# Double-buffered token tile, earlier layernorm and a later log/exp stage in an RWKV + FFN layer kernel

## The chip, the cores and the metric

One Trainium2 chip, 8 cores, one launch. Every core runs the same program on one sequence of the batch; the cores exchange nothing. The metric is the device time in microseconds of the slowest core, from the first to the last instruction with what little lies around them.

## The reference

Per sequence (4096 tokens of 1024 channels; the batch is 8), cut to what matters:

```python
xn = layernorm(x)                                  # over the 1024 channels, no scale or shift
k = xn @ Wk.T ; r = xn @ Wr.T ; v = r              # 1024 x 1024 each
y = wkv_scan(-exp(time_decay), time_first, k, v)   # recurrence over the tokens, per channel
attn = (sigmoid(r) * y) @ Wo.T
gate = xn @ (w_gate/127).T ; up = xn @ (w_up/127).T   # 3072 hidden, int32 weights
ffn = (silu(gate) * up) @ (w_down/127).T
out = x + attn + ffn
```

## The kernel before, in words

The program has two phases with a full barrier between them (`bd.fence()`). Phase 1 makes, for all tokens, the normalized input and the gated WKV output, and stores both to DRAM (`xn_s`, `outp_s`); it also transposes all weights and stores those of the FFN (`wgu_s`, `wdT_s`). Phase 2 (line 670 on, to L767) reads them back and does the FFN, the output projection and the sum. The change touches phase 1 alone.

There is no scheduler. `Build.op` appends each operation to the queue of its engine in the order in which the Python code calls it, and works out from the `Res` objects which semaphores it has to wait for. Each engine takes its own queue strictly in order, so a waiting instruction holds up all that stands behind it on that engine. The DMAs issued from SP stand in SP's queue in the same way, and those of GpSimd in POOL's; a DMA issue also waits for the last DMA on the same semaphore.

Phase 1 handles 16 chunks (`NC1`) of 256 tokens (`TT1`) in stages. For a chunk c:

- `stage_a_dma(c)`, L425: SP loads 1 MB of x into `x_tok`.
- `stage_a_stats(c)`: DVE takes BN_STATS and BN_AGGR (L433, L438) for two groups of 128 tokens, and ACT makes 1/sqrt(var+eps) as Ln and Exp of 128x1 (L443, L448). The second L438 writes the tile that the first L443 reads, so it waits for it.
- `stage_a_apply(c)`, L457: two DVE operations write the normalized bf16 tile `xn_tok` (a single buffer).
- `stage_a_post(c)`: TensorE transposes it into `psT` (L471, 16 transposes), ACT copies it to `xn_fm` (L478), SP stores it (L482). The text calls the 16 transposes T(c).
- `stage_b(c)`: TensorE makes k and r in four pairs of output blocks (L496). A pair is four groups of 8 matmuls, in the order psK, psR, psK, psR. `psK` and `psR` have two buffers each. Per pair ACT takes exp(k) (L506) and exp(-r) (L511), and DVE the product `S4` (L516), which sets `psR` free. At the end two small ACT copies (L526, L530).
- `stage_c_scans(c)`: 16 DVE scans (L540, L548). `stage_c_stt(c)`: 16 DVE operations (L561, L567) that make the denominator in `S6`.
- `stage_d(c)`: 16 ACT operations, Ln and Exp in turn (L576, L580), for the reciprocal of the denominator.
- `stage_e(c)`: 8 DVE operations (L590), one multiply on POOL into `outb` (L597), and the store of `outb` from SP (L603).

Beside the chunks, 64 units of weight preparation are dealt out, four per iteration, by `pp_drip`. A unit is a cast DMA from GpSimd into `pp_in` (two buffers), 8 transposes on TensorE (`psP`, L293, L321, L354), an ACT copy (L299 for Wo, L326 for gate and up, L360 for down) and, but for Wo, a store from `pp_stage` (two buffers) by SP (L331, L365). The load of a unit can be issued only when the transposes of the unit two before it are done, and an ACT copy into `pp_stage` waits for the store of the unit two before it. Units 0 to 7 are Wo (iterations 0 and 1), 8 to 55 gate and up (iterations 2 to 13), 56 to 63 down, with three groups of transposes and three copies each (iterations 14 and 15).

Iteration ch of the loop issues, in this order: the load for chunk ch+2, scans and stt of ch, stage e of ch-1, stage b of ch+1, stage d of ch, stats, apply and post of ch+2, and four units. T(2) is thus in iteration 0, T(15) in iteration 13, and from one T to the next are 13 intervals. Ahead of the loop stand stages a and b of chunk 0 and stage a of chunk 1.

Of the kernel before, what the change touches and what calls it, by code (L numbers as in the profile page):

```python
# [7 lines left out]
F32 = mybir.dt.float32  # L8
# [5 lines left out]
P = 128  # L14
C = 1024
# [108 lines left out]
def build_program(T=4096):  # L124
    TT1 = 256
    NC1 = T // TT1
    TS1 = TT1 // P
# [4 lines left out]
    nc = bass.Bass("TRN2", target_bir_lowering=False)  # L132
# [18 lines left out]
    bd = Build(nc)  # L151

    with contextlib.ExitStack() as top:
# [44 lines left out]
        with contextlib.ExitStack() as ph1:  # L198
            E1 = ph1.enter_context
            wkT = E1(nc.sbuf_tensor("wkT", [P, CC * C], BF16))  # L200
            wrT = E1(nc.sbuf_tensor("wrT", [P, CC * C], BF16))
            x_tok = [E1(nc.sbuf_tensor("x_tok0", [P, TS1 * C], F32))]
            xn_tok = [E1(nc.sbuf_tensor("xn_tok0", [P, TS1 * C], BF16))]
# [21 lines left out]
            r_wkT, r_wrT = Res("wkT"), Res("wrT")  # L225
            r_x_tok = [Res("x_tok0")]
            r_xn_tok = [Res("xn_tok0")]
# [11 lines left out]
            r_mv = [Res(f"mv{i}") for i in range(2)]  # L239
            r_stt = [Res(f"stt{i}") for i in range(2)]  # L240
# [15 lines left out]
            for i, v in [(0, EPS), (1, -0.5), (2, -1.0), (5, 127.0)]:  # L256
                bd.op("gpsimd", lambda e, i=i, v=v: e.memset(cst[:, i:i + 1], v),
                      writes=[r_cst])
# [162 lines left out]
            def stage_a_dma(ch):  # L421
                t0 = ch * TT1
                sl = ch % 2
                src = dram_ap(x_d, t0 * C, [[C, P], [P * C, TS1], [1, C]])
                bd.op("sync", lambda e, src=src: e.dma_start(out=x_tok[0][:], in_=src),  # L425
                      writes=[r_x_tok[0]], dma_sem="d_x0")

            def stage_a_stats(ch):
                sl = ch % 2
                for ts in range(TS1):  # L430
                    for hh in range(2):
                        bd.op("vector",
                              lambda e, sl=sl, ts=ts, hh=hh: e.bn_stats(  # L433
                                  stt_b[sl][:, (ts * 2 + hh) * 6:(ts * 2 + hh + 1) * 6],
                                  x_tok[0][:, ts * C + hh * 512: ts * C + (hh + 1) * 512]),
                              reads=[r_x_tok[0]], writes=[r_stt[sl]])
                    bd.op("vector",
# [15 lines left out]
            def stage_a_apply(ch):  # L453
                sl = ch % 2
                for ts in range(TS1):
                    bd.op("vector",
                          lambda e, sl=sl, ts=ts: e.tensor_scalar(  # L457
                              out=xn_tok[0][:, ts * C:(ts + 1) * C],
                              in0=x_tok[0][:, ts * C:(ts + 1) * C],
                              scalar1=mvb[sl][:, ts * 2:ts * 2 + 1], op0=ALU.subtract,  # L460
                              scalar2=rstd[sl][:, ts:ts + 1], op1=ALU.mult),
                          reads=[r_x_tok[0], r_mv[sl], r_rstd[sl]], writes=[r_xn_tok[0]])

# [141 lines left out]

            stage_a_dma(0)
            stage_a_stats(0)
            stage_a_apply(0)
            stage_a_post(0)
            stage_b(0)  # L610
            stage_a_dma(1)
            stage_a_stats(1)
            stage_a_apply(1)
            stage_a_post(1)
            while (pp_dma_idx < min(2, len(pp_units))
                   and pp_can_dma(pp_dma_idx, pp_idx)):
                pp_get(pp_dma_idx)[0]()
                pp_dma_idx += 1
            for ch in range(NC1):
                if ch + 2 < NC1:  # L620
                    stage_a_dma(ch + 2)
                stage_c_scans(ch, 0, CC)
                stage_c_stt(ch)
                if ch > 0:
                    stage_e(ch - 1)
                if ch + 1 < NC1:
                    stage_b(ch + 1)
                stage_d(ch)
                if ch + 2 < NC1:
                    stage_a_stats(ch + 2)  # L630
                    stage_a_apply(ch + 2)
                    stage_a_post(ch + 2)
                pp_drip((len(pp_units) * (ch + 1)) // NC1)
            stage_e(NC1 - 1)

# [171 lines left out]
```

How the kernel before makes its waits and increments, by code:

```python
        def emit(e, wl=wl, fn=fn, sem=sem, inc=inc):  # L77
            for s, v in wl:
                e.wait_ge(self.sems[s], v)
            inst = fn(e)
            inst.then_inc(self.sems[sem], inc)
# [10 lines left out]
        def emit(e, sem=sem, val=val):  # L92
            e.wait_ge(self.sems[sem], val)
```

## Time and profile before

| what | us |
|---|---|
| median of 3 runs | 2081.68 |
| lowest and highest | 2078.19, 2343.77 |
| the profiled execution, its own time | 2082.22 |
| its span on the slowest core (core 6) | 2080.7 |
| spans of the other seven cores | 2057.8 to 2078.0 |
| busy over the span: PE | 1537.6 (74%) |
| busy over the span: DVE | 629.4 (30%) |
| busy over the span: ACT | 465.4 (22%) |
| busy over the span: POOL | 122.3 (6%) |

The 1.5 us between the span and the execution's own time is what lies around the instructions. Busy shares are averages over two phases that have little in common: phase 1 takes the first 798 us or so, phase 2 the rest. The times of the rows below are microseconds from the start of the span. In a timeline a row is: start, duration, engine, line, operation, output and inputs, count, and in brackets the idle time of the engine before it with what ended it. PE is TensorE, DVE VectorE, ACT ScalarE, POOL GpSimd, SPq and POOLq the queues that issue DMAs.

### The profile page before, as it was taken

The page shows a single profiled execution, that of the slowest core. Times are in us where ns is not written, and L with a number is a line of the kernel's source. Part 1 is how long each engine was busy: PE and PEld are TensorE (multiplying, and loading weights), DVE is VectorE, ACT ScalarE, POOL GpSimd, SP SyncE. Part 2 cuts the span into 40 slices and gives each one's busy share as a digit, 9 for nine tenths or more (in the row PEclk, how much of TensorE's full clock was granted, in tenths as well). Part 3 has the DMA queues.
Part 4 walks back from the last instruction along what each step waited for, and adds up shares of the span by engine and source line. Part 5 has one row for each costly group of instructions (what it writes and reads, how often), then busy time and mean ns, then how long its engine had stood idle before and what let it go on. Part 6 is the DMA issues. An engine that isn't in the chain of part 4 may idle for free.

```text
span 2080.7 us, 24779 instructions; the slowest of 8 cores (2057.8 to 2080.7 us)
## 1 busy us (share of the span) xinstructions
PE 1537.6 (74%) x8192; PEld 801.9 (39%) x8192; DVE 629.4 (30%) x1094; ACT 465.4 (22%) x803; POOL 122.3 (6%) x112
## 2 busy tenths in 40 slices
PE   2554455446544423998998998998998998998995
PEld 2443444335444311433433433433433433433432
DVE  0455776676667510201201201201201201201201
ACT  3334444544443331100100100100100100100100
POOL 1011112112111110000000000000000000000000
PEclk9867678767777655999999999999999999999998
DMA  6323455355445477647647747647647648648641
GB/s 100 73 61 61 91 118 117 81 107 110 109 86 105 100 141 187 152 122 207 156 122 206 159 122 208 157 122 210 158 122 211 154 121 212 157 120 214 153 121 62
DMA packets 573611, 280.59 MB, mean 135 GB/s; under 512 B 477232, under 2 KB 526384, under 8 KB 573488
## 3 DMA queue, kind: packets, MB, share of 16 engines
q1 hardware_dynamic: 557744, 237.05, 45.1%
q0 software_dynamic: 15744, 41.95, 10.9%
q8 instruction: 71, 1.16, 0.2%
q14 instruction: 52, 0.43, 0.1%
HBM read 251.70 MB, written 52.43 MB: 146 GB/s over the span
## 4 chain that ended last, share of the span: by engine, by line
PE 71%; DMA 11%; ACT 7%; issue 6%; DVE 4%; SPq 0%; POOL 0%; ACTq 0%; DVEq 0%; POOLq 0%
PE psA L699 17%; PE psB L710 16%; PE psRb L740 9%; PE psR L496 6%; PE psK L496 6%; DMA pp_in<-wu 4%; PE psB L740 4%; PE psA L740 4%; PE psRb L752 3%; DMA pp_in<-wd 3%; ACT S L580 3%; ACT S L576 2%; DVE res L761 1%; PE psB L752 1%; PE psA L752 1%
## 5 line engine op out<-in xcount | busy, mean ns | idle before, releaser
L699 PE MATMUL psA<-xnc,wgu 128*128 128x512 bf16 x1536 | 375.6, 389 | 58.3 <-DVE res L761 29.6
L710 PE MATMUL psB<-xnc,wgu 128*128 128x512 bf16 x1536 | 367.4, 382 | 0.0
L718 ACT ACTIVATE sil<-psA,cst 128x512 f32<-128x512 f32 x192 | 131.9, 687 | 1036.2 <-PE psA L699 1036.2
L723 DVE SCALAR_TENSOR_TENSOR h_sb<-sil,cst,psB 128x512 bf16<-128x512 f32 x192 | 143.6, 748 | 597.8 <-PE psB L710 597.8
L699 PEld LDWEIGHTS psA<-xnc,wgu 128*128 128x128 bf16 x1536 | 152.3, 100 | 248.8 <-issue 75.1
L710 PEld LDWEIGHTS psB<-xnc,wgu 128*128 128x128 bf16 x1536 | 151.7, 99 | 186.7 <-issue 9.7
L740 PE MATMUL psRb<-wdt,h_sb 128*128 128x512 bf16 x768 | 196.4, 377 | 36.5 <-DVE h_sb L723 8.9
L761 DVE TENSOR_TENSOR res<-psRb,x 128x512 f32<-128x512 f32 x32 | 22.1, 692 | 525.6 <-PE psB L752 523.1
L471 PE MATMUL psT<-identsb,xn_tok 128*128 128x128 bf16 x256 | 29.8, 308 | 177.5 <-DVE xn_tok L457 177.5
L496 PE MATMUL psK<-xn_fm,wkT 128*128 128x256 bf16 x1024 | 150.2, 295 | 4.8 <-ACT xn_fm L478 3.1
L496 PE MATMUL psR<-xn_fm,wrT 128*128 128x256 bf16 x1024 | 145.9, 290 | 6.9 <-DVE S L516 6.9
L740 PEld LDWEIGHTS psRb<-wdt,h_sb 128*128 128x128 bf16 x768 | 61.4, 96 | 171.6 <-issue 125.7
L496 PEld LDWEIGHTS psK<-xn_fm,wkT 128*128 128x128 bf16 x1024 | 108.0, 106 | 24.8 <-issue 5.5
L496 PEld LDWEIGHTS psR<-xn_fm,wrT 128*128 128x128 bf16 x1024 | 106.4, 104 | 26.6 <-issue 8.0
L321 PE MATMUL psP<-identsb,pp_in 128*128 128x128 bf16 x384 | 46.8, 307 | 91.3 <-DMA pp_in<-wg 76.6
L740 PE MATMUL psB<-wdt,h_sb 128*128 128x512 bf16 x384 | 114.2, 379 | 0.0
L740 PE MATMUL psA<-wdt,h_sb 128*128 128x512 bf16 x384 | 114.2, 379 | 0.0
L471 PEld LDWEIGHTS psT<-identsb,xn_tok 128*128 128x128 bf16 x256 | 26.0, 142 | 181.5 <-issue 181.5
L540 DVE TENSOR_TENSOR_SCAN zDb<-dv,zDb,S 128x256 f32<-128x256 f32 x128 | 93.1, 728 | 0.0
L548 DVE TENSOR_TENSOR_SCAN zNb<-dv,zNb,S 128x256 f32<-128x256 f32 x128 | 92.8, 725 | 0.0
L516 DVE TENSOR_TENSOR S<-S,psR 128x512 f32<-128x512 f32 x64 | 43.8, 686 | 135.2 <-PE psK L496 81.3
L767 POOL DMA_DIRECT2D out<-res x8 | 6.0, 755 | 1277.3 <-DVE res L761 1277.3
(58 smaller groups left out, 1125.1 us busy)
## 6 DMA issues: line engine op xcount, KB each, us to landing
wgu<-wgu_s SPq DMA_DIRECT2D x192, 512.0 KB, 5.0
wdt<-wdT_s SPq DMA_DIRECT2D x192, 256.0 KB, 2.6
x_tok<-x SPq DMA_DIRECT2D x16, 1024.0 KB, 7.2
x<-x SPq DMA_DIRECT2D x8, 2048.0 KB, 15.5
out<-res POOLq DMA_DIRECT2D x8, 2048.0 KB, 8.6
wgu_s<-pp_stage SPq DMA_DIRECT2D x48, 256.0 KB, 6.0
xn_s<-xn_fm SPq DMA_DIRECT2D x16, 512.0 KB, 6.5
outp_s<-outb SPq DMA_DIRECT2D x16, 512.0 KB, 3.6
```

The costliest lines, as they stand in the source:

```text
L321: last = e.transpose(psP[sl][:, cc * P:(cc + 1) * P], pp_in[sl][:, cc * P:(cc + 1) * P], ident[:])
L471: last = e.transpose(psT[ts][:, cc * P:(cc + 1) * P], xn_tok[0][:, ts * C + cc * P: ts * C + (cc + 1) * P], ident[:])
L496: last = e.matmul(psx[pk][:, half * TT1:(half + 1) * TT1], wT[:, cc_i * C + cc_o * P: cc_i * C + (cc_o + 1) * P], xn_fm[sl][:, cc_i * TT1: ...
L540: lambda e, sl=sl, ol=ol, cc=cc, b0=b0: e.tensor_tensor_scan(out=zDb[sl][:, b0 + 1: b0 + 1 + TT1], data0=bass.AP(dv, cc, [[CC, P], [0, TT1]]),
L548: lambda e, sl=sl, ol=ol, cc=cc, b0=b0: e.tensor_tensor_scan(out=zNb[sl][:, b0 + 1: b0 + 1 + TT1], data0=bass.AP(dv, cc, [[CC, P], [0, TT1]]),
L580: lambda e, sl=sl, sli=sli: e.activation(out=S6[sl][:, sli], in_=S5[sl][:, sli], func=AF.Exp, scale=cst[:, 2:3]),
L699: last = e.matmul(psA[pab][:], wgu_t[wsl][:, (iu * CC + cc) * P:(iu * CC + cc + 1) * P], xnc[sl][:, cc * TT2:(cc + 1) * TT2], start=(cc == ...
L710: last = e.matmul(psB[pab][:], wgu_t[wsl][:, (iu * CC + cc) * P:(iu * CC + cc + 1) * P], xnc[sl][:, cc * TT2:(cc + 1) * TT2], start=(cc == ...
L718: lambda e, pab=pab: e.activation(out=sil_b[pab][:], in_=psA[pab][:], func=AF.Silu, scale=cst[:, 3:4]),
L723: lambda e, hc=hc, pab=pab: e.scalar_tensor_tensor(out=h_sb[:, hc * TT2:(hc + 1) * TT2], in0=sil_b[pab][:], scalar=cst[:, 4:5], in1=psB[pa ...
L740: last = e.matmul(bank_t[ts * 2 + dh][:], h_sb[:, hc * TT2 + ts * P: hc * TT2 + (ts + 1) * P], wd_t[wsl][:, dh * 512:(dh + 1) * 512], star ...
L752: last = e.matmul(bank_t[ts * 2 + dh][:], otc[sl][:, hc2 * TT2 + ts * P: hc2 * TT2 + (ts + 1) * P], woT[:, hc2 * C + dh * 512: hc2 * C + ( ...
```

## The change

`x_tok` gets a second buffer, with its own semaphore, and the load of x runs one chunk further ahead (ch+3 in iteration ch). In the loop, stats and apply of chunk ch+2 move from behind stage d to the head of the iteration, ahead of the scans; `stage_a_post(ch+2)` stays behind stage b; and stage d of ch moves from before them to the very end of the iteration, behind the four weight units.

```diff
-            x_tok = [E1(nc.sbuf_tensor("x_tok0", [P, TS1 * C], F32))]
+            x_tok = [E1(nc.sbuf_tensor(f"x_tok{i}", [P, TS1 * C], F32)) for i in range(2)]
...
-                bd.op("sync", lambda e, src=src: e.dma_start(out=x_tok[0][:], in_=src),
-                      writes=[r_x_tok[0]], dma_sem="d_x0")
+                bd.op("sync",
+                      lambda e, sl=sl, src=src: e.dma_start(out=x_tok[sl][:], in_=src),
+                      writes=[r_x_tok[sl]], dma_sem=f"d_x{sl}")
...
             stage_a_dma(0)
+            stage_a_dma(1)
             stage_a_stats(0)
             stage_a_apply(0)
             stage_a_post(0)
             stage_b(0)
-            stage_a_dma(1)
+            stage_a_dma(2)
             stage_a_stats(1)
             stage_a_apply(1)
             stage_a_post(1)
...
             for ch in range(NC1):
+                if ch + 3 < NC1:
+                    stage_a_dma(ch + 3)
                 if ch + 2 < NC1:
-                    stage_a_dma(ch + 2)
+                    stage_a_stats(ch + 2)
+                    stage_a_apply(ch + 2)
                 stage_c_scans(ch, 0, CC)
                 stage_c_stt(ch)
                 if ch > 0:
                     stage_e(ch - 1)
                 if ch + 1 < NC1:
                     stage_b(ch + 1)
-                stage_d(ch)
                 if ch + 2 < NC1:
-                    stage_a_stats(ch + 2)
-                    stage_a_apply(ch + 2)
                     stage_a_post(ch + 2)
                 pp_drip((len(pp_units) * (ch + 1)) // NC1)
+                stage_d(ch)
             stage_e(NC1 - 1)
```

The reads of `x_tok[0]` in stats and apply become reads of `x_tok[sl]` with sl the parity of the chunk. In the changed kernel lines behind L427 are numbered one higher, and those behind the loop three higher.

ScalarE's queue in the kernel before, around the end of iteration 1 and the start of iteration 2 (stage d is eight such pairs and four unit copies stand in a row, of which one pair and two copies are shown; the digit behind a name is the buffer):

```order
L576 ACTIVATE S5_1<-S6_1 128x256
L580 ACTIVATE S6_1<-S5_1,cst 128x256
L443 ACTIVATE lnv1<-mvb1,cst 128x1
L448 ACTIVATE rstd1<-lnv1,cst 128x1
L478 COPY xn_fm1<-psT0 128x8x128
L478 COPY xn_fm1<-psT1 128x8x128
L299 COPY woT<-psP0 128x8x128
L299 COPY woT<-psP1 128x8x128
L506 ACTIVATE S1_1<-psK0 128x512
```

ScalarE's queue in the changed kernel at the turn from one iteration to the next (L326 are the unit copies, L577 and L581 are stage d, L444 and L449 the Ln and Exp of the statistics, L507 is the first evacuation of stage b):

```order
L326 COPY pp_stage1<-psP0 128x1024
L326 COPY pp_stage0<-psP1 128x1024
L577 ACTIVATE S5_0<-S6_0 128x256
L581 ACTIVATE S6_0<-S5_0,cst 128x256
L444 ACTIVATE lnv1<-mvb1,cst 128x1
L449 ACTIVATE rstd1<-lnv1,cst 128x1
L507 ACTIVATE S1_0<-psK0 128x512
```

Before, stage d stood ahead of the statistics, the `xn_fm` copies and the units of its iteration; now it stands behind its iteration's units, and the statistics of the next iteration stand behind it.

VectorE's queue in the kernel before, at the turn from iteration 1 to iteration 2 (L590 is stage e of chunk 0, L516 the `S4` product of chunk 2, L433 to L457 the layernorm of chunk 3, L540 the first scan of chunk 2):

```order
L590 SCALAR_TENSOR_TENSOR S5_0<-S4_0,euv,zNb0 128x256 x8
L516 TENSOR_TENSOR S4_0<-S1_0,psR0 128x512
L516 TENSOR_TENSOR S4_0<-S1_0,psR1 128x512
L433 BN_STATS sttb1<-x_tok0 128x6 x2
L438 BN_AGGR mvb1<-sttb1 128x2
L457 TENSOR_SCALAR xn_tok0<-x_tok0,mvb1,rstd1 128x1024 x2
L540 SCALAR_TENSOR_TENSOR zDb0<-dv,zDb1,S1_0 128x256
```

VectorE's queue in the changed kernel, at the turn from iteration 2 to iteration 3 (L591 is stage e of chunk 1, L517 `S4` of chunk 3, L434 to L458 the layernorm of chunk 5, L541 the first scan of chunk 3):

```order
L591 SCALAR_TENSOR_TENSOR S5_1<-S4_1,euv,zNb1 128x256 x8
L517 TENSOR_TENSOR S4_1<-S1_1,psR0 128x512
L517 TENSOR_TENSOR S4_1<-S1_1,psR1 128x512
L434 BN_STATS sttb1<-x_tok1 128x6 x2
L439 BN_AGGR mvb1<-sttb1 128x2
L458 TENSOR_SCALAR xn_tok0<-x_tok1,mvb1,rstd1 128x1024 x2
L541 SCALAR_TENSOR_TENSOR zDb1<-dv,zDb0,S1_1 128x256
```

On VectorE the kinds of work follow each other as before; what differs is the chunk: the layernorm that stands ahead of the scans of chunk c is that of chunk c+2 instead of c+1.

## Rows read from the trace of the kernel before

**Rows 1.** Waits between 60 and 860 us: waiting, released by, total us, times, longest.

```profile
PE psT L471 <- DVE xn_tok L457: 172.6, 15, 12.0
ACT pp_stage L326 <- DMA wgu_s<-pp_stage: 123.1, 21, 8.2
```

**Rows 2.** Timeline of one iteration, all engines, 411 to 455 us.

```profile
411.25 1.73 DVE L457 TENSOR_SCALAR xn_tok<-x_tok,mvb,rstd 128x1024 bf16<-128x1024 f32 x2 [0.95 <-ACT rstd L448]
...
413.13 1.86 PE L471 MATMUL psT<-identsb,xn_tok 128*128 128x128 bf16 x16 [11.99 <-DVE xn_tok L457]
...
414.23 2.17 ACT L478 COPY xn_fm<-psT 128x1024 bf16<-128x1024 bf16 x2 [3.16 <-PE psT L471]
...
430.89 1.01 ACT L326 COPY pp_stage<-psP 128x1024 bf16<-128x1024 bf16 x1 [4.97 <-DMA wgu_s<-pp_stage]
...
433.80 0.68 DVE L516 TENSOR_TENSOR S<-S,psR 128x512 f32<-128x512 f32 x1
...
443.77 0.41 ACT L576 ACTIVATE S<-S 128x256 f32<-128x256 f32 x1
...
451.04 0.28 ACT L443 ACTIVATE lnv<-mvb,cst 128x1 f32<-128x1 f32 x1
...
452.71 1.73 DVE L457 TENSOR_SCALAR xn_tok<-x_tok,mvb,rstd 128x1024 bf16<-128x1024 f32 x2 [1.01 <-ACT rstd L448]
```

**Rows 3.** Busy time of each engine in the stretch 413.1 to 454.6 us.

```profile
413.10:454.60 41.50, 21.88 (x177) 18.55 (x178) 27.44 (x53) 18.71 (x36) 6.69 (x5) 0.71 0.47 102
```

**Rows 4.** Instructions on the tile x_tok: who waited, us in total, times.

```profile
DMA x_tok<-x: 13.3, 1
```

**Rows 5.** Timelines of PE and ACT: transposes of some chunks, with the iteration's last unit copy.

```profile
125.74 1.87 PE L471 MATMUL psT<-identsb,xn_tok 128*128 128x128 bf16 x16 [11.70 <-DVE xn_tok L457]
...
141.90 1.01 ACT L299 COPY woT<-psP 128x1024 bf16<-128x1024 bf16 x1 [4.36 <-PE psP L293]
...
253.00 1.86 PE L471 MATMUL psT<-identsb,xn_tok 128*128 128x128 bf16 x16 [11.70 <-DVE xn_tok L457]
...
266.64 1.01 ACT L326 COPY pp_stage<-psP 128x1024 bf16<-128x1024 bf16 x1 [2.10 <-DMA wgu_s<-pp_stage]
...
332.56 1.86 PE L471 MATMUL psT<-identsb,xn_tok 128*128 128x128 bf16 x16 [11.69 <-DVE xn_tok L457]
...
352.08 1.01 ACT L326 COPY pp_stage<-psP 128x1024 bf16<-128x1024 bf16 x1 [5.33 <-PE psK L496]
...
659.92 1.86 PE L471 MATMUL psT<-identsb,xn_tok 128*128 128x128 bf16 x16 [11.70 <-DVE xn_tok L457]
...
682.29 1.01 ACT L326 COPY pp_stage<-psP 128x1024 bf16<-128x1024 bf16 x1 [8.06 <-PE psR L496]
```

**Rows 6.** Timeline of iteration 0, 85 to 106 us.

```profile
85.13 1.73 DVE L457 TENSOR_SCALAR xn_tok<-x_tok,mvb,rstd 128x1024 bf16<-128x1024 f32 x2 [1.37 <-ACT rstd L448]
...
88.11 2.17 ACT L478 COPY xn_fm<-psT 128x1024 bf16<-128x1024 bf16 x2 [3.58 <-PE psT L471]
...
104.52 1.28 DVE L516 TENSOR_TENSOR S<-S,psR 128x512 f32<-128x512 f32 x2
```

**Rows 7.** Timeline of the end of phase 1, 691 to 794 us.

```profile
691.56 1.06 PE L354 MATMUL psP<-identsb,pp_in 128*128 128x128 bf16 x16
...
702.96 0.59 POOL L343 DMA_DIRECT2D pp_in<-wd  x1 [17.20 <-PE psP L354]
...
741.66 4.53 POOL L597 TENSOR_TENSOR outb<-S 128x2048 bf16<-128x2048 f32 x1
...
750.59 0.48 DVE L590 SCALAR_TENSOR_TENSOR S<-S,euv,zNb 128x256 f32<-128x256 f32 x1 [0.42 <-ACT S L580]
...
753.35 0.59 POOL L343 DMA_DIRECT2D pp_in<-wd  x1 [7.17 <-PE psP L354]
...
792.08 1.01 ACT L360 COPY pp_stage<-psP 128x1024 bf16<-128x1024 bf16 x1 [2.01 <-DMA wdT_s<-pp_stage]
793.73 0.48 SPq L603 DMA_DIRECT2D outp_s<-outb  x1
```

More of the change, by code:

```diff
@@ L225, in build_program @@
             r_wkT, r_wrT = Res("wkT"), Res("wrT")
-            r_x_tok = [Res("x_tok0")]
+            r_x_tok = [Res(f"x_tok{i}") for i in range(2)]
             r_xn_tok = [Res("xn_tok0")]
@@ L434, in stage_a_stats @@
                                   stt_b[sl][:, (ts * 2 + hh) * 6:(ts * 2 + hh + 1) * 6],
-                                  x_tok[0][:, ts * C + hh * 512: ts * C + (hh + 1) * 512]),
-                              reads=[r_x_tok[0]], writes=[r_stt[sl]])
+                                  x_tok[sl][:, ts * C + hh * 512: ts * C + (hh + 1) * 512]),
+                              reads=[r_x_tok[sl]], writes=[r_stt[sl]])
                     bd.op("vector",
@@ L458, in stage_a_apply @@
                               out=xn_tok[0][:, ts * C:(ts + 1) * C],
-                              in0=x_tok[0][:, ts * C:(ts + 1) * C],
+                              in0=x_tok[sl][:, ts * C:(ts + 1) * C],
                               scalar1=mvb[sl][:, ts * 2:ts * 2 + 1], op0=ALU.subtract,
                               scalar2=rstd[sl][:, ts:ts + 1], op1=ALU.mult),
-                          reads=[r_x_tok[0], r_mv[sl], r_rstd[sl]], writes=[r_xn_tok[0]])
+                          reads=[r_x_tok[sl], r_mv[sl], r_rstd[sl]], writes=[r_xn_tok[0]])
             def stage_a_post(ch):
```

## The prediction

> **What bounds the kernel now.** I read the rows in the order of the questions. First, who waits for whom in phase 1: the transposes of a chunk wait for the normalized tile for 172.6 us in 15 waits, and the unit copies of ScalarE wait for their stores for 123.1 us [rows 1]. The first looks like what the change goes for. Then one iteration in order of time shows why the transposes wait [rows 2]. After its last evacuation of stage b ScalarE runs stage d (from 443.77), and only behind it the Ln and Exp of the statistics (451.04). Apply follows at 452.71, the transposes at 454.59, and TensorE had been idle for 11.7 us before each T that I looked at [rows 5]. On VectorE the same row, apply, stands ahead of the scans, stt and stage e, and behind those stands the `S4` product that frees `psR` for the later pairs of stage b (433.80).
>
> So the loop that sets the period of 41 us is: apply, scans, stt, stage e, first `S4`, rest of stage b, stage d, Ln and Exp, apply. No engine is full: in 41.5 us PE is busy 21.88, DVE 27.44, ACT 18.71 (the PE, DVE and ACT entries of the row) [rows 3]. From T(2) at 125.74 to T(15) at 659.92 are 13 intervals, 534.2 us, 41.1 each [rows 5].
>
> **The x tile.** On `x_tok` somebody waited once in the whole run, 13.3 us, for the first load [rows 4]. The second buffer and the earlier issue therefore remove nothing, and the load costs nothing on SP: it is issued at the same place as before, behind the last `wgu_s` store of an iteration, and its buffer has been free since the apply of an iteration earlier. I take 0. The first load would still have to land, so the 13.3 us stay. The Trainium skill, in Trainium Kernel Development and Optimization, section Best Practices, says to double-buffer so that DMA overlaps with compute. By that rule this edit would gain time; the trace has no such wait to remove after the first, so it changes nothing.
>
> **What the reordering removes.** T(ch+2) no longer waits for apply, which has run an iteration's length earlier. It starts when stage b ends. That takes 11.7 us of idle time from TensorE. But nothing downstream is bound by that alone.
>
> **What it adds.** The Ln and Exp of the next layernorm now stand behind stage d on ScalarE, and stage d stands behind the four unit copies. On VectorE the scans still stand behind apply. So scans(ch+1) wait for: T(ch+2), its copies, the four units with their DMAs, stage d(ch), Ln and Exp of ch+3, apply(ch+3). Before, the units ran beside the 22 us of scans, stt and stage e; that cover is gone, since VectorE stands idle until the units and stage d are done. And stage b of ch+2 can do two of its four pairs and then waits in `psR` for `S4`, which waits for all of it. Everything behind it waits too: the next T, and with it the next units. I add up the interval from T to T:
>
> - From T to the end of the last unit copy. In [rows 5]: 141.90+1.01-125.74 = 17.2 for the first iteration; 14.65 is the least of 13 (253.00 to 267.65), 20.5 the largest (332.56 to 353.09). The mean of iterations 0 to 12 is 18.4, and the iteration of [rows 2] has 18.8. The long part is DMA: the loads of the last two units can only be issued when the first two have been transposed, and the last copy waits for the store of the second unit [rows 2]. These transfers stand in the same order in both kernels. I take 18.4.
> - Stage d: 443.77 to 451.04, 7.3 [rows 2].
> - Ln, Exp and the ping-pong with BN_AGGR: 451.04 to 452.71, 1.7 [rows 2].
> - Apply, scans, stt and stage e, up to the first `S4`: 411.25 to 433.80, 22.5 [rows 2].
> - From the first `S4` to the end of stage b, where TensorE has stood at `psR`: iteration 0 of the kernel before has such a case. `S4` starts at 104.52 [rows 6], and stage b ends at 125.74-11.70 = 114.04 [rows 5]: 9.5.
>
> The sum is 59.4 us against 41.1, 18.3 us more in each of 13 intervals: +238.
>
> **Ahead of them.** In iteration 0 statistics and apply of chunk 2 come between apply(1) and the first scan. ScalarE is busy with the copies of T(1) until 88.11+2.17 = 90.3; then come 1.7 for Ln and Exp and 1.65 for apply, so the scans start at 93.6. Before, they started at 85.13+1.65 = 86.8 [rows 6]. Stage b(1) ends 6.8 later, at 120.8, and T(2) stands there instead of at 125.74: -4.9.
>
> **Behind them.** After T(15) there is no apply. In iteration 13 the last unit copy ended 23.4 after T [rows 5]. Stage d(13) then runs to 30.7; stage e(13) writes what it reads and so ends with it; exp(k) and exp(-r) of the first pair, half the width of a unit copy each and so some 0.65 us by estimate, take 1.3 more; 9.5 to the end of b(15): 41.5, where it was 691.56-659.92 = 31.6 [rows 5, 7]. In exchange stage d(14) no longer stands ahead of the first copies of unit 56, whose following load was issued 11.4 after stage b ended (702.96) [rows 7] and now some 4.1 after by estimate (three groups of transposes and a copy at 1.0 each [rows 7]): at 45.6 instead of 43.0 after T(15), +2.5. Stage d(14) falls into the wait for the load of unit 60, at the place where d(15) stood before (to 750.5), but the POOL multiply of chunk 14 now follows it: 751.1+0.2+4.53 = 755.8, and the load behind it on POOL's queue, issued at 753.35 before, goes out 2.6 later [rows 7]. Last, d(15) stands bare at the end: from 793.1 on 7.3 of stage d, 0.6 for the last L590, 4.7 for the multiply, 0.3 to the issue: the last `outp_s` store is issued at 806.0 instead of 793.73 [rows 7], +12.3, and the barrier to phase 2 waits for it. Together +17.4. Phase 2 is the same code and gets the same inputs: 0.
>
> **Sum.** -4.9 + 238 + 17.4 = +250.5 on the profiled execution's 2082.2, which lies 0.5 above the median of the runs shown: 2333.
>
> **Rivals.**
> - The transfers shrink. The 18.4 us are mostly waits for DMA, and with a longer interval the queues could be emptier, so that four copies of 1.0 follow the `xn_fm` copies (which end at 416.40, 3.3 after T [rows 2]) at once: 7.3 in place of 18.4. Then an interval is 48.3 and the kernel 2333-13x11.1 = 2189, still slower. Against it: these DMAs wait for each other within one iteration, which a longer interval does not change. 7 in 100.
> - The period stays at 41.1 and the idle time only moves from T to `psR`: 2082-4.9+17.4 = 2095, within 2%. It would need scans that don't wait for the late Ln and Exp. The queue of VectorE speaks against it: apply stands ahead of the first scan. 3 in 100.
> - Faster. If stage d ran inside the waits of ScalarE between the unit copies, the 11.7 us of TensorE would go and nothing take their place: 13x11.7 = 152 less, 2082-5-152+17 = 1942. For it speaks that no engine is over 27.44 busy in 41.5 [rows 3]; against it, ScalarE takes its queue in order and stage d is behind the copies. 2 in 100.
> - The forecast, in which ScalarE's queue ties units and scans into one loop, holds 88 in 100. It costs time from the point where T to last copy is longer than 41.1-41.0 = 0.1 us (41.0 is the sum of the other four terms), so no shortening of the transfers alone can turn it.
>
> **How the numbers follow.** The unknown is how long the units take in the new rhythm. With the least value (14.65) in each interval the sum falls by 13x3.7 = 49 to 2284; with the largest (20.5) it rises by 28 to 2361, and with the 23.4 of iteration 13 by 65 to 2398. The range is 2275 to 2385. A measurement of this kernel can tell about 2% from no change; by the cases faster is 0.02, the same 0.03, slower 0.95.
>
> **What would show it.** In the changed profile the wait of L472 for `xn_tok` should be gone; T to T should be 57 to 62 us; VectorE should stand some 20 us idle ahead of the second BN_AGGR (L439), released by ScalarE; ScalarE's first evacuation L507 should follow L449 directly; TensorE should have two idle stretches, for the unit loads and over 20 us at psR (L497) for `S4`. Phase 2 should keep its length. I am wrong if L439 waits only a few us, if intervals are under 50, or if the last unit copy comes under 10 us after T.

## The result, and the profile after

The changed kernel takes 2318.47 us in the median of 10 runs (lowest 2299.62), the kernel before 2081.65 us. The ratio is 1.1098 with a 95% interval from 1.1054 to 1.1143: 11% slower. The profiled execution has a span of 2298.1 us on its slowest core (core 4) against 2080.7. Most kernels here have some runs that are disturbed and far longer; the ratios leave them out, the medians do not.

The difference of 217.4 us between the two spans lies in phase 1. The starts of the transposes T and the first load of phase 2 cut both profiles into the same parts:

| part | before | after | difference | predicted |
|---|---|---|---|---|
| start to T(2) | 125.7 | 124.2 | -1.5 | -4.9 |
| T(2) to T(15), 13 intervals | 534.2 | 743.4 | +209.2 | +238 |
| T(15) to the first load of phase 2 | 138.4 | 148.5 | +10.2 | +17.4 |
| phase 2 | 1282.4 | 1282.0 | -0.4 | 0 |

Before, an interval was 41.1 us; now it is 57.2. First the waits of the changed kernel between 60 and 1030 us (waiting, released by, us in total, times, longest), which answer to [rows 1]:

```profile
PE psR L497 <- DVE S L517: 289.1, 14, 22.3
DVE mvb L439 <- ACT lnv L444: 247.3, 14, 20.4
...
ACT pp_stage L326 <- DMA wgu_s<-pp_stage: 108.0, 20, 6.1
PE psK L497 <- ACT S L507: 105.5, 14, 8.9
...
PE psT L472 <- DVE xn_tok L458: 13.4, 2, 8.5
```

The wait of the transposes for the normalized tile is gone, as intended: 13.4 us in two waits, both ahead of the loop, where there were 172.6 in 15. In its place TensorE waits 289 us for `S4` to free `psR`, in 14 waits of up to 22.3, and VectorE 247 us for the Ln of the statistics. The wait of the unit copies for their stores is about as long as before (108.0 against 123.1). It is the same wait, and yet it now costs what it did not cost then, since VectorE stands idle behind it.

The timeline of one interval of the changed kernel, which answers to [rows 2]:

```profile
577.68 1.06 PE L472 MATMUL psT<-identsb,xn_tok 128*128 128x128 bf16 x16
...
578.73 2.17 ACT L479 COPY xn_fm<-psT 128x1024 bf16<-128x1024 bf16 x2
...
593.64 1.01 ACT L326 COPY pp_stage<-psP 128x1024 bf16<-128x1024 bf16 x1 [3.96 <-PE psK L497]
...
594.54 0.42 ACT L577 ACTIVATE S<-S 128x256 f32<-128x256 f32 x1
...
601.82 0.28 ACT L444 ACTIVATE lnv<-mvb,cst 128x1 f32<-128x1 f32 x1
...
602.26 0.21 DVE L439 BATCH_NORM_AGGREGATE mvb<-sttb 128x2 f32<-128x12 f32 x1 [19.40 <-ACT lnv L444]
603.02 0.29 ACT L449 ACTIVATE rstd<-lnv,cst 128x1 f32<-128x1 f32 x1
603.22 0.58 ACT L507 ACTIVATE S<-psK 128x512 f32<-128x512 f32 x1
...
603.91 1.73 DVE L458 TENSOR_SCALAR xn_tok<-x_tok,mvb,rstd 128x1024 bf16<-128x1024 f32 x2 [1.43 <-ACT S L507]
...
626.46 1.28 DVE L517 TENSOR_TENSOR S<-S,psR 128x512 f32<-128x512 f32 x2
...
627.28 1.86 PE L497 MATMUL psR<-xn_fm,wrT 128*128 128x256 bf16 x8 [21.48 <-DVE S L517]
...
635.49 1.06 PE L472 MATMUL psT<-identsb,xn_tok 128*128 128x128 bf16 x16
```

Read from top to bottom it is the loop of the prediction. The transposes start without idle time ahead of them. The last unit copy ends 17.0 us later (594.65), stage d runs 7.2 us behind it, Ln, aggregate and Exp 2.1, and only then does apply run. VectorE has stood still for 19.4 us at the second BN_AGGR, and ScalarE's first evacuation (603.22) follows the last Exp of the statistics directly. The first `S4` comes 22.55 after apply begins, TensorE has been waiting 21.48 us in `psR`, and 9.0 us after `S4` starts the next transposes begin. 17.0 + 7.2 + 2.1 + 22.55 + 9.0 adds up to this interval, 57.8 with the second decimals.

The busy time of each engine over the 13 intervals (stretch, its length, then PE, PEld, DVE, ACT, POOL busy with their counts, the granted clock of TensorE as a share, DMA share, GB/s), first of the kernel before and then of the changed one:

```profile
125.70:659.90 534.20, 275.98 (x2288) 236.51 (x2289) 356.55 (x677) 242.63 (x468) 86.98 (x65) 0.74 0.47 99
```

```profile
124.20:867.60 743.40, 293.93 (x2290) 232.62 (x2289) 355.00 (x676) 237.65 (x469) 86.91 (x65) 0.68 0.32 70
```

VectorE's work is the same in both, 357 and 355 us. No engine is busy longer but PE, by 18 us for the same instructions: its granted clock fell from 0.74 to 0.68 in the mean. Behind the wait of 21.48 us in `psR` the clock is at the lower of its two levels (1.2 GHz) for most of the next 4.7 us and then at the upper one (2.4 GHz); the granted clock is the third entry from the end, 0.54 and 1.00:

```profile
627.30:632.00 4.70, 4.70 (x25) 3.33 (x25) 0.44 (x1) 0.60 (x1) 3.96 (x1) 0.54 0.00 0
632.00:635.50 3.50, 3.50 (x35) 3.14 (x33) 0.69 (x1) 1.28 (x2) 0.00 (x0) 1.00 0.51 154
```

TensorE's work behind the first `S4` is part of the loop, and the 9.0 us hold these slower rows, as the 9.5 of the forecast did. The rest of the loss is idle time.

### The profile page after: what moved, and what is told of

It reads as the page before. It is cut to its first block, busy times and chain, and to the rows that moved or that the text cites. A ratio compares the mean times of both kernels' runs of the same rounds, so it can differ in the third digit from the quotient of the medians.

```text
span 2298.1 us, 24717 instructions; the slowest of 8 cores (2287.1 to 2298.1 us)
## 1 busy us (share of the span) xinstructions
PE 1548.6 (67%) x8089; PEld 797.8 (35%) x8192; DVE 627.7 (27%) x1094; ACT 460.4 (20%) x803; POOL 122.2 (5%) x112
## 3 DMA queue, kind: packets, MB, share of 16 engines
q1 hardware_dynamic: 557744, 237.05, 40.4%
## 4 chain that ended last, share of the span: by engine, by line
PE 59%; DMA 12%; DVE 11%; issue 10%; ACT 7%; POOL 0%; DVEq 0%; ACTq 0%; SPq 0%; POOLq 0%
PE psA L702 15%; PE psB L713 15%; PE psRb L743 8%; DMA wgu_s<-pp_stage 5%; PE psR L497 4%; PE psB L743 4%; PE psA L743 3%; PE psK L497 3%; PE psRb L755 3%; ACT S L581 2%; DVE S L562 2%; DVE S L568 2%; ACT S L577 2%; DMA pp_in<-wd 2%; DVE S L591 2%
## 5 line engine op out<-in xcount | busy, mean ns | idle before, releaser
L497 PE MATMUL psR<-xn_fm,wrT 128*128 128x256 bf16 x1024 | 164.2, 314 | 289.1 <-DVE S L517 289.1
L497 PE MATMUL psK<-xn_fm,wkT 128*128 128x256 bf16 x1024 | 172.9, 325 | 108.6 <-ACT S L507 105.5
L497 PEld LDWEIGHTS psR<-xn_fm,wrT 128*128 128x128 bf16 x1024 | 113.8, 112 | 322.0 <-issue 294.8
L497 PEld LDWEIGHTS psK<-xn_fm,wkT 128*128 128x128 bf16 x1024 | 117.2, 116 | 142.2 <-issue 112.6
L743 PEld LDWEIGHTS psRb<-wdt,h_sb 128*128 128x128 bf16 x768 | 61.4, 96 | 171.6 <-issue 125.7
L507 ACT ACTIVATE S<-psK 128x512 f32<-128x512 f32 x64 | 37.9, 593 | 392.8 <-PE psK L497 392.8
L598 POOL TENSOR_TENSOR outb<-S 128x2048 bf16<-128x2048 f32 x16 | 72.0, 4502 | 539.6 <-DVE S L591 539.6
L541 DVE TENSOR_TENSOR_SCAN zDb<-dv,zDb,S 128x256 f32<-128x256 f32 x128 | 93.1, 727 | 0.0
L439 DVE BATCH_NORM_AGGREGATE mvb<-sttb 128x2 f32<-128x12 f32 x32 | 6.7, 209 | 289.8 <-ACT lnv L444 288.0
L321 PE MATMUL psP<-identsb,pp_in 128*128 128x128 bf16 x384 | 36.8, 262 | 67.3 <-DMA pp_in<-wg 56.2
L517 DVE TENSOR_TENSOR S<-S,psR 128x512 f32<-128x512 f32 x64 | 42.7, 684 | 142.4 <-PE psK L497 89.8
```

Source lines behind the costliest of these rows:

```text
L497: last = e.matmul(psx[pk][:, half * TT1:(half + 1) * TT1], wT[:, cc_i * C + cc_o * P: cc_i * C + (cc_o + 1) * P], xn_fm[sl][:, cc_i * TT1: ...
L541: lambda e, sl=sl, ol=ol, cc=cc, b0=b0: e.tensor_tensor_scan(out=zDb[sl][:, b0 + 1: b0 + 1 + TT1], data0=bass.AP(dv, cc, [[CC, P], [0, TT1]]),
L598: bd.op("gpsimd", lambda e, sl=sl: e.tensor_tensor(out=outb[0][:], in0=S5[sl][:], in1=S6[sl][:], op=ALU.mult), reads=[r_s5[sl][cc] for cc ...
L743: last = e.matmul(bank_t[ts * 2 + dh][:], h_sb[:, hc * TT2 + ts * P: hc * TT2 + (ts + 1) * P], wd_t[wsl][:, dh * 512:(dh + 1) * 512], star ...
```

## The experiments

All kernels were timed beside the kernel before on the same chip. T to T below is (T(15)-T(2))/13 in each profile.

**The buffer alone.** The kernel before with the second `x_tok` and the earlier load; the two lines ahead of the loop are as in the change.

```diff
 # the order of the kernel before, but:
-                if ch + 2 < NC1:
-                    stage_a_dma(ch + 2)
+                if ch + 3 < NC1:
+                    stage_a_dma(ch + 3)
                 stage_c_scans(ch, 0, CC)
```

> The kernel before with the second x_tok buffer and the load one chunk further ahead, nothing else moved. Loop theory (the loss comes from the order on ScalarE and VectorE, not from the buffer): period stays 41 us, the start is some 3 us longer because two loads of x now stand beside the first weight loads; 2082 to 2090 us. Rival (the extra early load contends with the unit transfers in each iteration): over 2110.

Measured: median 2084.15 us, ratio 1.0004 (0.9980 to 1.0029), T to T 41.1. The buffer and the load gain and cost nothing that can be measured; the transposes wait as before (the 16th wait is T(0), which lies ahead of the window in the kernel before):

```profile
PE psT L472 <- DVE xn_tok L458: 177.5, 16, 12.0
```

**Stage d put back.** The changed kernel, with stage d behind stage b again.

```diff
                 if ch + 1 < NC1:
                     stage_b(ch + 1)
+                stage_d(ch)
                 if ch + 2 < NC1:
                     stage_a_post(ch + 2)
                 pp_drip((len(pp_units) * (ch + 1)) // NC1)
-                stage_d(ch)
```

> The changed kernel with stage d put back where it stood before (behind stage b, ahead of post and the units); statistics and apply stay at the head of the iteration. Loop theory (it is the Ln and Exp behind the four unit copies that closes the loop, wherever stage d stands on ScalarE in between): from the end of stage b 1.2 + stage d 7.3 + xn_fm copies and units up to some 24.5, Ln and Exp 1.7, 22.5 to the first S4, 9.5 to the end of stage b: a period of 58, 2290 to 2330 us. Rival (the late stage d is the cause): back to 2085 or less.

Measured: 2252.99 us, ratio 1.0844 (1.0801 to 1.0886), T to T 54.7. The late stage d is not the main cause: without it most of the loss, 8.4 of 11.0%, is still there, and VectorE still waits for the Ln and TensorE for `S4` (between 60 and 1000 us):

```profile
PE psR L497 <- DVE S L517: 288.9, 15, 22.3
DVE mvb L439 <- ACT lnv L444: 212.8, 14, 19.1
```

My number missed: I had expected 58, not 54.7. The miss lies in one term: from the end of stage b to the last unit copy I took 24.5 us, with stage d and the units as a plain sum, and in the profile it is 21.2 in the mean of the 13 intervals. Part of stage d lies beside transfers: the loads of the last two units are issued at its start, while the first copies, and the stores behind them, still wait for its end. T is at 554.10, stage d runs from 555.14 to 562.52, and the last copy ends 23.2 after T:

```profile
555.14 0.42 ACT L577 ACTIVATE S<-S 128x256 f32<-128x256 f32 x1
556.14 0.59 POOL L313 DMA_DIRECT2D pp_in<-wg  x1 [6.58 <-PE psP L321]
556.73 0.54 POOL L313 DMA_DIRECT2D pp_in<-wu  x1
...
576.27 1.01 ACT L326 COPY pp_stage<-psP 128x1024 bf16<-128x1024 bf16 x1 [5.95 <-DMA wgu_s<-pp_stage]
```

**Statistics and apply put back behind stage b.** Stage d stays at the very end.

```diff
-                if ch + 2 < NC1:
-                    stage_a_stats(ch + 2)
-                    stage_a_apply(ch + 2)
                 stage_c_scans(ch, 0, CC)
...
                 if ch + 2 < NC1:
+                    stage_a_stats(ch + 2)
+                    stage_a_apply(ch + 2)
                     stage_a_post(ch + 2)
```

> The changed kernel with statistics and apply put back behind stage b and ahead of post; stage d stays at the very end. Loop theory: Ln and Exp stand ahead of the units again and no longer behind stage d, so T comes 8.5 us after stage b instead of 11.7; the scans run beside the units; but stage d and then the first evacuation follow the last unit copy: 8.5 + 17.6 + 7.3 + 1.3 to the first S4, then 9.5, a period of 44; about 2135 us (2110 to 2155). Rival (late stage d is the cause of the whole loss): about 2310. Rival (the early layernorm alone is the cause and stage d is free): 2045 or so, since T comes 3 us sooner.

Measured: 2138.28 us, ratio 1.0176 (1.0131 to 1.0221), T to T 42.9 where I had expected 44 (1.0176 of before is 2118). T comes 8.2 us after stage b instead of 11.7, and stage d at the end delays the first `S4`. The two together make an interval 1.8 us longer than in the kernel before, 23 us in all, and from T(15) to the first load of phase 2 it takes 153.8 us instead of 138.4. So a stage d behind the units costs something by itself, even where the scans run beside the units, but it is the small part.

**Statistics and apply ahead of the units.** VectorE's and TensorE's orders are those of the changed kernel; on ScalarE the two pairs of Ln and Exp pass the units and stage d.

```diff
-                if ch + 2 < NC1:
-                    stage_a_stats(ch + 2)
-                    stage_a_apply(ch + 2)
                 stage_c_scans(ch, 0, CC)
...
                 if ch + 2 < NC1:
                     stage_a_post(ch + 2)
+                if ch + 3 < NC1:
+                    stage_a_stats(ch + 3)
+                    stage_a_apply(ch + 3)
```

(with statistics and apply of chunk 2 ahead of the loop)

> The changed kernel with one thing moved: statistics and apply of a chunk stand directly behind post of the chunk before it, ahead of the four units, instead of behind units and stage d. VectorE's order stays exactly as in the changed kernel, TensorE's too; only on ScalarE Ln and Exp pass the units and stage d. Loop theory: apply some 7 us after stage b ends, 22.5 to the first S4, 9.5 to the end of stage b: a period of 39, about 2060 us (2035 to 2085), so the whole loss goes. Rivals (late stage d, or the early layernorm on VectorE, or the load of x is the cause): 2200 or more.

Measured: 2064.74 us, ratio 0.9912 (0.9872 to 0.9952), T to T 38.2. Four operations of 0.3 us, put elsewhere in one queue, take the whole loss away and a little more: 37 us less in the 13 intervals than in the kernel before, of which 18 are lost again behind T(15). The waits between 60 and 860 us:

```profile
PE psR L497 <- DVE S L517: 42.6, 12, 12.0
...
DVE mvb L439 <- ACT lnv L444: 0.5, 1, 0.5
```

Of VectorE's 247.3 us of waiting for the Ln 0.5 are left, and of TensorE's 289.1 in `psR` 42.6.

**The scans first.** The changed kernel with VectorE's order alone changed; ScalarE's is that of the changed kernel.

```diff
-                if ch + 2 < NC1:
-                    stage_a_stats(ch + 2)
-                    stage_a_apply(ch + 2)
                 stage_c_scans(ch, 0, CC)
                 stage_c_stt(ch)
                 if ch > 0:
                     stage_e(ch - 1)
+                if ch + 2 < NC1:
+                    stage_a_stats(ch + 2)
+                    stage_a_apply(ch + 2)
```

> The changed kernel with VectorE's order alone changed: statistics and apply of chunk ch+2 stand behind stage e(ch-1) instead of ahead of the scans. ScalarE's and TensorE's orders stay as in the changed kernel, Ln and Exp still behind the units and stage d. Loop theory (both halves are needed: Ln and Exp behind the units on ScalarE and the scans behind apply on VectorE): the scans run beside the units again; stage e ends with stage d, 25.5 after T, then statistics 3.7, Ln and Exp and apply 3.4, the first S4, 9.5 to the end of stage b: a period of 42 to 43, about 2110 us (2085 to 2130). Rival (ScalarE's order alone makes the loss): 2300.

Measured: 2083.28 us, ratio 1.0028 (1.0005 to 1.0051), T to T 40.4. ScalarE's queue still has Ln and Exp behind the units and stage d, and yet nearly all of the loss is gone. So both halves are needed: the late Ln on ScalarE, and on VectorE an apply that the scans stand behind. What is left shows as a wait of TensorE for ScalarE's first evacuation (between 60 and 860 us):

```profile
PE psK L497 <- ACT S L507: 176.0, 15, 14.2
```

The time was expected at about 2110 us, 1.4% more than before, and the loss is 0.3%, just under the expected 2085 to 2130. T to T was put at 42 to 43: I had counted 9.5 us from the first `S4` to the next T, from a TensorE that has stood in `psR`. Here it took 7.8 (480.31 to 488.08 in the profile). TensorE had begun a group of the third pair at 479.04, ahead of `S4`; the group behind `S4` takes 1.87 us, the next 1.09 and the others 1.04, where the changed kernel has 1.86, 1.91, 1.51 and then 1.04.

**A third staging buffer**, in the changed kernel and in the kernel before; nothing else differs but the list of semaphores, which is longer to match.

```diff
-                ssl = pp_mat_unit.ctr % 2
+                ssl = pp_mat_unit.ctr % 3
...
-                        ssl = (ctr + g) % 2
+                        ssl = (ctr + g) % 3
...
-            pp_stage = [E1(nc.sbuf_tensor(f"pp_stage{i}", [P, C], BF16)) for i in range(2)]
+            pp_stage = [E1(nc.sbuf_tensor(f"pp_stage{i}", [P, C], BF16)) for i in range(3)]
-            r_pp_stage = [Res(f"pp_stage{i}") for i in range(2)]
+            r_pp_stage = [Res(f"pp_stage{i}") for i in range(3)]
```

> The changed kernel with three pp_stage buffers instead of two, nothing moved: the last unit copy of an iteration no longer waits for the store of the second unit. In the changed kernel that wait is 3.9 to 5.2 us in each of the 12 iterations with gate and up units. Loop theory (the units' transfers are a term of the period): the last copy comes some 5 us earlier after T, the period falls from 57.8 to 53 in some 11 intervals, 55 us less: about 2250 (2235 to 2270). Rival (the units lie beside other work and only stage d or the layernorm counts): 2300 to 2310, unchanged.

> The kernel before with the same third pp_stage buffer. The unit copies have the scans, stt and stage e of VectorE as cover there, and only the first evacuation of stage b stands behind them, with a few us to spare: 2075 to 2085 us, within 0.3% of before. Were the units on the path of the kernel before too, it would gain as much as the changed kernel, 2030.

Measured: the changed kernel with the third buffer has a ratio of 1.0751 (1.0725 to 1.0777) to the kernel before, where the changed kernel had 1.1098: 72 us less, at about 2236. T to T fell from 57.2 to 52.8, which is 57 us in the 13 intervals where 55 were expected; another 8 lie behind T(15). In the kernel before the same buffer changed nothing that can be measured: its lowest run is 2077.95 beside 2076.23 of the kernel before (there is no ratio on record), and T to T is 41.0. The wait that the buffer was to remove is nearly gone in both. The wait of the unit copies in the kernel before with a third buffer, between 60 and 860 us, and then in the changed kernel with it, between 60 and 1030:

```profile
ACT pp_stage L326 <- DMA wgu_s<-pp_stage: 3.4, 1, 3.4
```

```profile
ACT pp_stage L326 <- DMA wgu_s<-pp_stage: 24.0, 9, 3.8
```

From 123.1 to 3.4 us in the one, with no gain, and from 108.0 to 24.0 in the other, with 72 us of gain. Part of that wait only got another name, since the copies then wait for the units' loads (in the kernel before 78.5 us for the transposes behind them). What counts is the end of the last unit copy after T. It came 3.9 us earlier in the kernel before (14.5 instead of 18.4 in the mean of 13 intervals) and 4.5 earlier in the changed kernel (12.1 instead of 16.6). An interval shortened by 0.1 us in the one and by 4.4 in the other. One interval of the kernel before with the third buffer:

```profile
415.22 1.86 PE L471 MATMUL psT<-identsb,xn_tok 128*128 128x128 bf16 x16 [11.99 <-DVE xn_tok L457]
...
427.93 1.01 ACT L326 COPY pp_stage<-psP 128x1024 bf16<-128x1024 bf16 x1 [2.06 <-PE psP L321]
```

This shows most directly that the units' transfers lay beside VectorE's work before and lie in the loop now.

**Two interleaved versions**, meant to beat both kernels. Both start from the kernel before, with a single `x_tok`; stages b, d, e, scans and stt take a range of blocks. The first:

```diff
-                stage_c_scans(ch, 0, CC)
-                stage_c_stt(ch)
-                if ch > 0:
-                    stage_e(ch - 1)
+                for pr in range(4):
+                    ccs = (2 * pr, 2 * pr + 1)
+                    if ch > 0:
+                        stage_e(ch - 1, ccs, tail=(pr == 3))
+                    if ch + 1 < NC1:
+                        stage_b(ch + 1, (pr,), tail=False)
+                    stage_c_scans(ch, 2 * pr, 2 * pr + 2)
+                    stage_c_stt(ch, ccs)
+                    if pr > 0:
+                        stage_d(ch, (2 * pr - 2, 2 * pr - 1))
+                    pp_drip(4 * ch + pr + 1)
                 if ch + 1 < NC1:
-                    stage_b(ch + 1)
-                stage_d(ch)
+                    stage_b(ch + 1, (), tail=True)
                 if ch + 2 < NC1:
                     stage_a_stats(ch + 2)
                     stage_a_apply(ch + 2)
                     stage_a_post(ch + 2)
-                pp_drip((len(pp_units) * (ch + 1)) // NC1)
+                stage_d(ch, (6, 7))
```

> A version meant to beat both: the single x_tok buffer, and per iteration four quarters, each with two blocks of stage e(ch-1), one pair of stage b(ch+1), scans, stt of two blocks of ch, stage d of the two blocks before and one weight unit; then statistics, apply and post, and the last quarter of stage d. No engine takes a whole stage before the next, so VectorE no longer waits for the pairs of stage b, and the waits for the unit transfers are spread. By the loop view the period comes near VectorE's 27.4 us busy plus the few us around the layernorm, 31 to 35: 13 x 8 = 104 less, about 1970 (1930 to 2010). If instead the unit transfers (loads and stores of four units, some 17 us in a chain) bound an iteration, or the quarters wait on each other across ScalarE, 2050 to 2100.

Measured: 2160.15 us, ratio 1.0128 (1.0069 to 1.0186; 1.0128 of before is 2107), T to T 44.3. A miss of the other sign: expected 1970, it is slower than the kernel before. One iteration in its timeline:

```profile
417.76 4.49 POOL L599 TENSOR_TENSOR outb<-S 128x2048 bf16<-128x2048 f32 x1 [9.93 <-DVE S L590]
418.32 4.48 DVE L540 TENSOR_TENSOR_SCAN zDb<-dv,zDb,S 128x256 f32<-128x256 f32 x1
...
431.14 1.74 DVE L457 TENSOR_SCALAR xn_tok<-x_tok,mvb,rstd 128x1024 bf16<-128x1024 f32 x2 [0.95 <-ACT rstd L448]
...
433.02 1.86 PE L471 MATMUL psT<-identsb,xn_tok 128*128 128x128 bf16 x16 [22.34 <-DVE xn_tok L457]
...
436.44 1.86 PE L496 MATMUL psK<-xn_fm,wkT 128*128 128x256 bf16 x8 [1.55 <-ACT xn_fm L478]
...
443.72 0.69 DVE L516 TENSOR_TENSOR S<-S,psR 128x512 f32<-128x512 f32 x1 [10.05 <-ACT S L511]
```

Statistics, apply and T came last in the iteration, and stage b of that very chunk stood at the head of the next: T, copies, first pair and first `S4` lay in a row with nothing beside them. TensorE waits 22.34 us for apply and VectorE then 10.05 for the pair. I had closed a new loop of the same kind as the change. The rows show a second cost: the scan at 418.32, beside POOL's multiply, took 4.48 us instead of 0.73 (see the last section). Between the first `S4` of the iteration (399.45) and apply (431.14) VectorE waits for 1.5 us in all, so these 3.75 us lie in the loop. Without them an interval would have some 40.6 us by estimate, half a microsecond under the 41.1 of the kernel before: the new loop took the gain away, and the slowed scan makes up the loss. The second version, as a difference to the first, takes the loop apart:

```diff
                 for pr in range(4):
                     ccs = (2 * pr, 2 * pr + 1)
+                    stage_c_scans(ch, 2 * pr, 2 * pr + 2)
+                    stage_c_stt(ch, ccs)
                     if ch > 0:
                         stage_e(ch - 1, ccs, tail=(pr == 3))
                     if ch + 1 < NC1:
                         stage_b(ch + 1, (pr,), tail=False)
-                    stage_c_scans(ch, 2 * pr, 2 * pr + 2)
-                    stage_c_stt(ch, ccs)
                     if pr > 0:
                         stage_d(ch, (2 * pr - 2, 2 * pr - 1))
+                    if ch + 2 < NC1 and pr == 1:
+                        stage_a_stats(ch + 2)
+                    if ch + 2 < NC1 and pr == 2:
+                        stage_a_apply(ch + 2)
+                        stage_a_post(ch + 2)
                     pp_drip(4 * ch + pr + 1)
                 if ch + 1 < NC1:
                     stage_b(ch + 1, (), tail=True)
-                if ch + 2 < NC1:
-                    stage_a_stats(ch + 2)
-                    stage_a_apply(ch + 2)
-                    stage_a_post(ch + 2)
                 stage_d(ch, (6, 7))
```

> The interleaved version mended in two places that its trace showed: in each quarter scans, stt and stage e come ahead of the pair of stage b (there the first S4 of an iteration waited 10 us for a pair that had just been started), and statistics, apply and post of ch+2 stand in the second and third quarter, so that the transposes no longer come last and stage b of the next chunk follows at once (TensorE waited 22 us for them). VectorE's work is 27.4 us per iteration, with up to 4 more where its scans stand beside the POOL multiply: a period of 31 to 35 and about 1975 us (1940 to 2015). If the unit transfers or waits between the quarters on ScalarE bind: 2030 or more.

Measured: 1977.51 us, ratio 0.9490 (0.9437 to 0.9542), T to T 35.5, just above the 31 to 35 expected. It beats the kernel before by 5% and the changed kernel by 14%. Over its 13 intervals (columns as in the windows above):

```profile
115.20:576.90 461.70, 253.47 (x2288) 220.43 (x2289) 357.00 (x675) 235.75 (x468) 82.03 (x64) 0.78 0.55 115
```

VectorE has the same 357 us of work, now in 461.7, and is busy for 77% of the stretch instead of 48% in the changed kernel. In this order no scan begins while the multiply runs. Three things differ from the first version (the scans ahead of the pair, the place of the layernorm and the transposes, and with them the scan beside the multiply), and no run tells their shares apart.

## Why the prediction was right, and where its sizes were off

The forecast was 2333 us with a range of 2275 to 2385; measured is 2318. By its own steps:

- **The x tile, 0.** Right inside the loop: the buffer alone gives 1.0004, and T to T stays at 41.1. At the start there is a small cost that the step did not name. The load of the second chunk now stands beside the first weight loads, and T(0) starts at 62.8 instead of 59.4. In the seven profiles with two early loads it starts at 61.0 to 64.5, in the four with one load at 58.4, 59.4, 59.6 and 62.1; the two groups overlap, so that the load is what delays it is likely but not shown. By T(1) the delay is 4.6 us (91.6 instead of 87.0), and from T(1) to T(2) it takes 32.6 us where the step had 33.8. The two add up to a T(2) at 124.2 and not at 120.8. In the run with the buffer alone the whole time shows no such cost that can be measured.
- **What the reordering removes, 11.7 us of TensorE waiting per iteration.** Right, and worth nothing by itself, as was said.
- **What it adds.** Right in its mechanism. Each half was taken away alone, the late Ln (0.9912) and the scans behind apply (1.0028), and each alone removes the loss. The third term, the transfers of the units, was shown by the staging buffer.
- **The sum of an interval, 59.4 against 57.2 measured.** The term that was too large is the one from T to the last unit copy: 18.4 was taken, and the mean of the 13 intervals is 16.6, 24 of the 29 us by which the 13 intervals were over-predicted. It splits in two. In iterations 2 to 12 the copy ends 17.0 to 17.8 after T instead of 14.7 to 20.5, 1.0 less in the mean; no run shows why. In iterations 0 and 1, where the units are Wo and have no store, it ends after 11.6 and 11.1 instead of 17.2 and 17.7. I had written that these transfers stand in the same order in both kernels, and for iteration 0 that was wrong. TensorE comes straight from stage b, and its 16 transposes take 1.06 us instead of 1.86. So POOL issues the two weight loads at 126.28, ahead of the `xn_s` store (127.58) and the load of x (128.10) on SP's queue; before, they were issued at 129.00 and 129.86, level with those two (129.15 and 129.66). The rows of the changed kernel, POOL's and SP's timeline:

```profile
126.28 1.08 POOL L285 DMA_DIRECT2D pp_in<-Wo  x2 [67.26 <-PE psP L293]
```

```profile
127.58 0.37 SPq L483 DMA_DIRECT2D xn_s<-xn_fm  x1
128.10 0.75 SPq L426 DMA_DIRECT2D x_tok<-x  x1
```

  That the loads are faster because they were issued first is argued from these times and was not tried by itself.
- **The other terms.** From the first `S4` to the next T 9.5 was taken, and it is 9.0 in the interval shown, because T now follows the last matmul directly, while the 9.5 ran to the modelled end of stage b. Ln, Exp and the ping-pong with BN_AGGR took 2.1 instead of 1.7. Stage d (7.2 for 7.3) and apply to `S4` (22.55 for 22.5) were as taken.
- **The end, +17.4 against +10.2.** The bare stage d(15) at the end was right: from the last unit copy to the last `outp_s` issue 12.6 us instead of 0.6, as forecast. What was too large is the step before: I took 23.4 us from T to the last unit copy of iteration 13, a single case of the kernel before, and it was 18.4; stage b(15) ended 35.2 after T and not 41.5. The last unit copy ends 132.0 us after T(15), 1.2 less than before, where the forecast had 5.1 more. The last row of the units, then stage d, the multiply and the store:

```profile
998.58 1.01 ACT L360 COPY pp_stage<-psP 128x1024 bf16<-128x1024 bf16 x1 [1.97 <-DMA wdT_s<-pp_stage]
999.49 0.42 ACT L577 ACTIVATE S<-S 128x256 f32<-128x256 f32 x1
...
1007.66 4.49 POOL L598 TENSOR_TENSOR outb<-S 128x2048 bf16<-128x2048 f32 x1 [21.64 <-DVE S L591]
1012.23 0.36 SPq L604 DMA_DIRECT2D outp_s<-outb  x1
```

- **Phase 2, 0.** Right, -0.4 us.

Of the rivals, the shrinking transfers were partly true: 1.8 us per interval, not 11.1. The sentence in the forecast that stage d is part of what the loop adds up was right for this kernel, but the experiment with stage d put back shows that its place is the smaller part: 7.3 us moved out of there brought only 2.5 per interval.

## What to carry to other kernels

A wait that is the longest in the list is not thereby the one that sets the time. Before moving work up to remove it, follow the moved instruction onto each in-order queue that it issues on, and write down the whole loop from an event to the same event one iteration later; here a 0.3 us Ln on ScalarE, now behind four units of weight preparation, stood between one iteration of VectorE's work and the next. A stall costs nothing while another engine works beside it: unit copies that ended some 4 us earlier in each iteration gained nothing in one order and 72 us in the other. Small pieces of each stage in turn are not enough by themselves: the first interleaved version lost 1.3%. The one that gained 5% also made the result that the next iteration begins on well before the end of its own.

## What the runs showed of the hardware

In the first interleaved version a scan of VectorE over 128x256 elements took 4.48 us instead of the usual 0.73, in each of the 13 iterations where it began while POOL's 4.5 us multiply was running (4.42 us in one of them): POOL from 417.76 to 422.25, the scan from 418.32 to 422.80. VectorE's busy time over that whole run is 678.9 us, against 629.4 in the kernel before and 630.7 in the second interleaved version:

```profile
PE 1538.1 (73%) x8192; PEld 790.4 (37%) x8192; DVE 678.9 (32%) x1094; ACT 467.4 (22%) x803; POOL 121.4 (6%) x112
```

The extra 49.5 us are about 13 times the 3.75 us of that scan's excess, so a wait for the other engine is hidden in a duration and shows in no list of waits. In the second interleaved version the `S4` product, with one input in PSUM, keeps its 0.69 us beside the multiply. The Trainium skill says this in SBUF — State Buffer, section Who interferes with whom (for the port pair that VectorE and GpSimd share): a VectorE operation with two inputs in SBUF and a GpSimd operation that reads SBUF exclude each other, and the second to issue blocks until the first has finished. This trace agrees, with 4.48 us for a scan, whose inputs `zDb`, `dv` and `S` are all in SBUF, that began 0.56 us after a multiply of 4.49.
